# Second layer's expert feed-forward: tokens sorted through DRAM into 23 blocks, one expert each

## What is computed

```python
def _L1_ffn_ref(x, switch_w, switch_b, w1, b1, w2, b2):
    t = x.reshape(-1, d)                                # 2048 tokens of 128
    route_prob = jax.nn.softmax(t @ switch_w + switch_b, axis=-1)
    route_prob_max = jnp.max(route_prob, axis=-1)
    routes = jnp.argmax(route_prob, axis=-1)
    for e in range(8):                                  # w1[e]: 128 x 512, w2[e]: 512 x 128
        h = jax.nn.gelu(t @ w1[e] + b1[e])
        y = h @ w2[e] + b2[e]
        out = jnp.where((routes == e)[:, None], y, out)
    return out * route_prob_max[:, None]
```

## Time and profile before

| what | value |
|---|---|
| time, median of 3 runs | 1949.45 us (1949.03 to 1950.55) |
| profiled execution: span of its instructions | 1948.2 us |
| median less that span | 1.25 us |
| TensorE busy | 1760.2 us, 90% |
| VectorE busy | 1222.4 us, 63% |
| ScalarE busy | 966.7 us, 50% |
| POOL busy | 265.7 us, 14% |
| mean granted TensorE clock | 0.972 of 2.4 GHz |
| chain that ended last | TensorE 65%, VectorE 18%, ScalarE 7%, issue 7% |
| transfers, whole run | 21.09 MB, 3.6% of the sixteen DMA engines' time |

### The profile page before, as it was taken

The page is one execution under the profiler, slowest core; times in us unless marked ns, Lnnn a source line. Parts: engine busy times, 40 slices in busy tenths (PEclk is TensorE's granted clock), DMA queues, the critical chain, the costliest instruction groups (busy, mean ns, idle before and its releaser), DMA issues.

```text
span 1948.2 us, 40574 instructions
## 1 busy us (share of the span) xinstructions
PE 1760.2 (90%) x14281; PEld 1350.1 (69%) x14281; DVE 1222.4 (63%) x3198; ACT 966.7 (50%) x2010; POOL 265.7 (14%) x358
## 2 busy tenths in 40 slices
PE   4999999989997899988999977999968999999987
PEld 3788888866664688875777754666646777777775
DVE  5966666667665678884222246555555778777781
ACT  1566666654332567775444343323314556555552
POOL 2000000011002143321000014000010011111111
PEclk9999999999998899998999989999978999999999
DMA  8000000000002000000000010000000000000000
GB/s 251 1 1 0 0 0 0 0 2 1 1 0 64 27 1 0 0 1 1 1 1 0 0 51 1 1 1 0 0 0 1 1 1 0 0 0 0 0 1 22
DMA packets 19157, 21.09 MB, mean 11 GB/s; under 512 B 4650, under 2 KB 14003, under 8 KB 18884
## 3 DMA queue, kind: packets, MB, share of 16 engines
q1 hardware_dynamic: 19076, 20.02, 3.6%
HBM read 18.97 MB, written 1.05 MB: 10 GB/s over the span
## 4 chain that ended last, share of the span: by engine, by line
PE 65%; DVE 18%; ACT 7%; issue 7%; POOL 1%; SPq 1%; DMA 0%; DVEq 0%; ACTq 0%; POOLq 0%
PE bank L1152 56%; PE bank L1156 9%; DVE PTs L1754 2%; DVE negm L1745 2%; DVE negm L1750 2%; ACT Pm L1053 2%; DVE Qz L1949 2%; ACT VxF L1010 1%; ACT PTs L1009 1%; ACT Pm L1113 1%; DVE Qz L1549 1%; DVE VxF L604 1%; DVE st L1557 1%; DVE On L1810 1%; SPq L699 1%
## 5 line engine op out<-in xcount | busy, mean ns | idle before, releaser
L1152 PE MATMUL bank<-kT,Qz 128*128 128x256 f32 (+1 forms) x1568 | 442.3, 387 | 4.0 <-issue 1.6
L1053 ACT ACTIVATE Pm<-bank,negm 128x256 f32<-128x256 f32 x784 | 326.7, 468 | 207.0 <-DVE negm L1750 206.3
L1152 PE MATMUL bank<-xH,R 128*128 (+3 forms) x928 | 299.6, 382 | 13.5 <-DVE Qz L1949 13.4
L1152 PEld LDWEIGHTS bank<-R,Qz 128*128 128x128 f32 (+1 forms) x2496 | 293.8, 192 | 17.8 <-ACT Qz L1120 6.4
L1152 PE MATMUL bank<-R,Qz 128*128 128x128 f32 (+1 forms) x2496 | 295.2, 276 | 3.1 <-ACT Qz L1120 3.1
L1152 PEld LDWEIGHTS bank<-kT,Qz 128*128 128x128 f32 x1568 | 248.9, 192 | 67.9 <-issue 16.9
L1156 PE MATMUL bank<-ident,Pm 128*128 128x128 f32 x1568 | 239.1, 275 | 50.6 <-DVE PTs L1754 40.6
L1754 DVE TENSOR_TENSOR PTs<-bank,PTs 128x512 f16<-128x512 f32 x384 | 261.9, 682 | 7.7 <-ACT PTs L1009 7.2
L1156 PEld LDWEIGHTS bank<-ident,Pm 128*128 128x128 f32 x1568 | 187.2, 141 | 113.3 <-issue 59.2
L1750 DVE TENSOR_REDUCE negm<-bank 128x2 f32<-128x512 f32 x264 | 181.6, 688 | 95.6 <-PE bank L1152 91.7
L1009 ACT ACTIVATE PTs<-bank 128x512 f16<-128x512 f32 (+1 forms) x388 | 231.3, 596 | 3.1 <-PE bank L1156 3.1
(11 more groups left out here) (231 smaller groups left out, 2085.1 us busy)
## 6 DMA issues: line engine op xcount, KB each, us to landing
R<-in_L_ffn_ew SPq DMA_DIRECT2D x2, 1024.0 KB, 6.9
R<-in_L_ffn_w SPq DMA_DIRECT2D x1, 2048.0 KB, 9.8
R<-in_L_xattn_Wkv SPq DMA_DIRECT2D x2, 768.0 KB, 6.5
R<-in_L_ffn_w SPq DMA_DIRECT2D x1, 1408.0 KB, 12.9
R<-in_L_xattn_Wq SPq DMA_DIRECT2D x2, 512.0 KB, 3.7
out<-x SPq DMA_DIRECT2D x4, 256.0 KB, 2.3
PTs<-in_ctx SPq DMA_DIRECT2D x1, 768.0 KB, 8.1
R<-in_L_xattn_Wo SPq DMA_DIRECT2D x1, 512.0 KB, 7.8
```

The lines of the kernel that those rows point to most:

```text
L1053: last = act.activation(Pm[:, k % 4, qt * S:(qt + 1) * S], bank[k % 2][:, qt * S:(qt + 1) * S], ACT.Exp, bias=negm[:, k % 4, qt:qt + 1])
L1152: return pe.matmul(o, l, r, start=start, stop=stop)
```

## The change

The second layer's feed-forward (`ROUTED = (1,)`) no longer follows `ffn_schedule`. Each engine gets a function `routed` that runs once for all 2048 tokens:

1. Each attention sequence's normalised rows are also copied by POOL, unturned, to `xrow` (which takes the memory of `xH` and `xL`; the split of this layer's inputs goes).
2. TensorE makes the gate for all four chunks; VectorE finds each token's expert as a one-hot row. TensorE counts, with an upper triangular matrix and sums over tiles, each token's rank among those of its expert. VectorE rounds each expert's count up to whole blocks of 128 and so gets each token's slot, and each block's expert. 2048 tokens make at most 16 + 7 = 23 blocks.
3. The down bias is added for all tokens, through TensorE, into `x`. VectorE then takes the third layer's maxima (`layer2_scale`).
4. POOL scatters the 16 tiles of rows to DRAM (`xs`), by slot, in 16 indirect transfers.
5. SP loads the sorted rows block by block, up to eight ahead. For each block TensorE turns the rows, ScalarE and VectorE split them into f16 parts, TensorE multiplies them by the weights of the block's expert, ScalarE applies bias and gelu, TensorE makes the down product, VectorE copies it out, and SP stores it to DRAM (`ys`). The expert's number is loaded to a register of TensorE and of ScalarE, and the addresses of weights and bias are computed from it.
6. When all blocks are stored, POOL gathers 16 tiles of rows back by slot, VectorE adds them with the token's weight to `x`, and statistics, normalisation and turn go by chunks.

Around it: DRAM rows are zeroed by ten writes of 256 KB on SP's queue in the beginning, and POOL sets some more constants there. The third layer's `early` waits for the routed stage's semaphores.

```diff
+ROUTED = (1,)
+RING = 8
+def n_blocks(F):
+    return NT * F.k + 7
...
@@ sync
+            sp.wait_ge(consts_ready, 2)
+            for i in range(10):
+                sp.dma_start(xs[512 * i:512 * i + 512, :].rearrange("(t p) d -> p t d", p=P),
+                             wpad[:, :, :]).then_inc(rows_zeroed, 16)
...
+                def load_block(i):
+                    sp.wait_ge(r.turned, i - RING + 1) if i >= RING else None
+                    sp.dma_start(xb[:, i % RING, :], xs[i * P:(i + 1) * P, :]).then_inc(r.loaded[i % RING], 16)
+                sp.wait_ge(r.scattered, 16 * NT * F.k)
+                for i in range(RING):
+                    load_block(i)
+                for i in range(nb):
+                    sp.wait_ge(r.y_read, i + 1)
+                    sp.dma_start(ys[i * P:(i + 1) * P, :], yb[:, i % RING, :]).then_inc(r.stored[i % RING], 16)
+                    if i + RING < nb:
+                        load_block(i + RING)
@@ gpsimd, attention
+                    if A.n in ROUTED:
+                        need(pool, s.yn, b + 1)
+                        pool.tensor_copy(xrow[:, bass.ds(2 * b, 2), :], yn[:, 0:2, :]).then_inc(routed_s[A.n].rows, 1)
@@ gpsimd, feed_forward
+                if F.n in ROUTED:
+                    pool.memset(Vx2[:, :, 128], 1.0).then_inc(zeroed, 1)
+                    largest(2)
+                    routed(F)
+                    return
...
+            def routed(F):
+                pool.wait_ge(r.rows, B)
+                pool.wait_ge(r.slots, 1)
+                for t in range(NT):
+                    pool.indirect_dma_start(out=xs, out_offset=bass.IndirectOffsetOnAxis(ap=slotu[:, t:t + 1], axis=0),
+                                            in_=xrow[:, t, :], in_offset=None).then_inc(r.scattered, 16)
+                for j in range(RING):
+                    pool.wait_ge(r.stored[j], 16 * ((nb - j + RING - 1) // RING))
+                def gather(t):
+                    if t >= RING:
+                        pool.wait_ge(r.added, t - RING + 1)
+                    pool.indirect_dma_start(out=yg[:, t % RING, :], out_offset=None, in_=ys[0:nb * P, :],
+                                            in_offset=bass.IndirectOffsetOnAxis(ap=slotu[:, t:t + 1], axis=0)
+                                            ).then_inc(r.gathered[t % RING], 16)
+                for t in range(RING):
+                    gather(t)
+                for c in range(NCH):
+                    need(pool, s.lnf, c + 1)
+                    need(pool, s.stats, c + 1)
+                    normalise(4, s.stats, c + 1, s.yn, 1.0, EPS, link)
+                    for t in range(RING + 4 * c, min(RING + 4 * c + 4, NT)):
+                        gather(t)
@@ scalar, per block
+                        move(xbH[:, i % 4, :], bank[6 + i % 2][:, 0:P]).then_inc(r.high, 1)
+                    if i >= 1:
+                        j = i - 1
+                        e = act.value_load(blocke[0:1, j:j + 1], min_val=0, max_val=7)
+                        act.wait_ge(r.h, j + 1)
+                        for ft in range(F.FT):
+                            last = act.activation(sg[:, j % 4, ft * P:(ft + 1) * P],
+                                                  bank[j % 2][:, ft * P:(ft + 1) * P], ACT.Gelu_apprx_tanh,
+                                                  bias=vecT[:, bass.ds(e * 4 + (V_B1 + ft), 1)],
+                                                  scale=upback[:, 1:2])
@@ tensor
+                need(pe, att_s[F.n].yn, B)
+                for t in range(2):
+                    last = turn(bank[6][:, t * P:(t + 1) * P], yn[:, t, :])
+                last.then_inc(s.lnf.sem, 1)
...
+                def up_block(i):
+                    e = expert[i] = pe.value_load(blocke[0:1, i:i + 1], min_val=0, max_val=7)
+                    pe.wait_ge(r.high, i + 1)
+                    pe.wait_ge(r.low, i + 1)
...
+                    for ft in range(F.FT):
+                        o = bank[i % 2][:, ft * P:(ft + 1) * P]
+                        w = [r1h[:, bass.ds(e * 1024 + (512 * j + ft * P), P)] for j in range(2)]
+                        mm(o, w[0], xbH[:, i % 4, :], True, False)
+                        mm(o, w[0], xbL[:, i % 4, :], False, False)
+                        last = mm(o, w[1], xbH[:, i % 4, :], False, True)
+                def down_block(i):
+                    pe.wait_ge(r.g, i + 1)
+                    for ft in range(F.FT):
+                        last = mm(bank[4 + i % 2][:, 0:P], sg[:, i % 4, ft * P:(ft + 1) * P],
+                                  R1[:, bass.ds(e * 512 + (4608 + ft * P), P)], ft == 0, ft == F.FT - 1)
+                turn_block(0)
+                for i in range(nb + 1):
+                    if i + 1 < nb:
+                        turn_block(i + 1)
+                    if i < nb:
+                        up_block(i)
+                    if i:
+                        down_block(i - 1)
@@ vector
+                for c in range(NCH):
+                    dve.wait_ge(r.bias, c + 1)
+                    dve.tensor_tensor(x[:, 4 * c:4 * c + 4, :], bank[c % 2][:, :].rearrange("p (t d) -> p t d", d=D),
+                                      x[:, 4 * c:4 * c + 4, :], ALU.add).then_inc(r.bias_added, 1)
+                layer2_scale()
+                for i in range(nb + 1):
+                    if i < nb:
+                        dve.wait_ge(r.high, i + 1)
+                        dve.tensor_tensor(xbL[:, i % 4, :], bank[6 + i % 2][:, 0:P], xbH[:, i % 4, :],
+                                          ALU.subtract).then_inc(r.low, 1)
+                    if i:
...
+                        dve.tensor_copy(yb[:, j % RING, :], bank[4 + j % 2][:, 0:P]).then_inc(r.y_read, 1)
```

More of the change, by code:

```diff
@@ L66, in __init__ @@
         self.ctxb, self.qm, self.ostats, self.onorm = c["ctxb"], c["qm"], c["ostats"], c["onorm"]
+class RoutedSems:
+    def __init__(self, sem, n):
+        self.gate, self.gate_read, self.logits = sem(f"r{n}_gate"), sem(f"r{n}_gate_read"), sem(f"r{n}_logits")
+        self.onehot, self.rank, self.slots = sem(f"r{n}_onehot"), sem(f"r{n}_rank"), sem(f"r{n}_slots")
+        self.experts, self.shifted, self.exped = sem(f"r{n}_experts"), sem(f"r{n}_shifted"), sem(f"r{n}_exped")
+        self.w, self.wT, self.wT_read = sem(f"r{n}_w"), sem(f"r{n}_wT"), sem(f"r{n}_wT_read")
+        self.bias, self.bias_added = sem(f"r{n}_bias"), sem(f"r{n}_bias_added")
+        self.rows, self.scattered = sem(f"r{n}_rows"), sem(f"r{n}_scattered")
+        self.loaded = [sem(f"r{n}_loaded{j}") for j in range(RING)]
+        self.turned, self.high, self.low = sem(f"r{n}_turned"), sem(f"r{n}_high"), sem(f"r{n}_low")
+        self.h, self.g, self.y, self.y_read = sem(f"r{n}_h"), sem(f"r{n}_g"), sem(f"r{n}_y"), sem(f"r{n}_y_read")
+        self.stored = [sem(f"r{n}_stored{j}") for j in range(RING)]
+        self.gathered = [sem(f"r{n}_gathered{j}") for j in range(RING)]
+        self.added = sem(f"r{n}_added")
 class FeedForwardSems:
@@ L574, in build, with splits_before @@
                  counted(list(ffn_counts(FFN[0])), "ffn_", [ffn_counts(F) for F in FFN])]
+        routed_s = {n: RoutedSems(sem, n) for n in ROUTED}
+        def splits_before(n):
+            return sum(NCH for m in range(n) if m not in ROUTED)
         Vx2 = VxF[:, 0:16 * 129].rearrange("p (t e) -> p t e", e=129)
@@ L794, in _ @@
             pool.memset(mb3[:, :], 0.0)
-            pool.memset(wpad[:, :, :], 0.0)
+            pool.memset(onehot[:, :, :], 0.0)
+            pool.memset(before128[:, :, :], 128.0)
             for e in range(8):
                 pool.memset(iota[:, e:e + 1], float(e))
+                pool.memset(rev[:, e:e + 1], 8.0 - e)
+            for i in range(40):
+                pool.memset(step128[:, i:i + 1], 128.0 * i)
+            link(pool.memset(under[:, :], 1.0))
+            link(pool.affine_select(out=under[:, :], in_=under[:, :], compare_op=ALU.is_ge, fill=0.0,
+                                    base=-1, pattern=[[1, P]], channel_multiplier=-1))
+            pool.affine_select(out=before128[:, :, :], in_=before128[:, :, :], compare_op=ALU.is_ge, fill=0.0,
+                               base=-1, pattern=[[1, 8], [-1, 8]], channel_multiplier=0)
             link(pool.memset(headmask[:, :], 1.0))
@@ L880, in body @@
                             normalise(2, s.stats, h + 1, s.yn, 1.0, EPS, link, 2 * (h % 2))
-                            if h == 5:
+                            if h == 5 and A.n not in ROUTED:
                                 split_inputs(0)
@@ L904, in body @@
                         largest(A.n)
-                    if A.n < 2 and kinds == "last":
+                    if A.n < 2 and A.n not in ROUTED and kinds == "last":
                         m = [m for kind, k, m, _ in steps(A, b, kinds) if kind in FILLS][0]
@@ L1257, in attention @@
                     need(pe, f.lne, NCH)
-                    need(pe, f.gle, NCH)
-                    if FFN[A.n - 1].k == 1:
```

(19 more changed lines are left out.)

215 lines of the change are left out of this document (208 added, 7 removed).

## The result

The changed kernel takes 1907.38 us (median of 4 runs, 1906.42 to 1908.51), the kernel before 1950.0 beside it; the ratio is 0.978, 95% interval 0.977 to 0.980. Forecast were 1898, its own range 1880 to 1920, the wide one 1862 to 1942. The profiled execution has a span of 1904.9 us.

The account below looks back on a forecast made before the run. TensorE, nearly without a gap from 890.1 to 1114.86 us, was taken as the bound. Eleven dependent steps end at 1063.5, 51.4 sooner: 1949.45 - 51.4 + 0.3 = 1898.4, so 1898 us, range 1880 to 1920.

Parts of the forecast that it names:

- Steps 1 to 3: Stage start: last normalisation with gate products queued behind the turn, +4.4; gate, +8.1; routing on VectorE and TensorE, +7.8 us.
- Step 4: Down bias through TensorE: 1.9 us a chunk plus 1.5 of fill, +9.1 us.
- Step 5: Next layer's scale: POOL's reduction, behind VectorE's maxima, stands ahead of the scatter; 6.07 + 0.15, then 2.8, +9.1 us.
- Step 6: Scatter: 16 indirect transfers from POOL at 1.2 us each, 19.2, and 2.0 to land, +21.2 us.
- X: Price of one indirect transfer on POOL: taken as 1.2 us, from 0.79 for its own pass and 0.43 for an issue.
- cheap transfers: Rival: POOL's indirect transfer costs as an SP issue, 0.43 us, so 25 us less, 1873; chance 24%.
- slower case: Rival on POOL's queue: above 2.8 us per indirect transfer the change loses, at 3.34 the time is 1966; chance 11%.
- Step 8: Block loop: 23 blocks at 3.0 us, 69 plus 2.5 for fill and drain, +71.5 us.
- ScalarE's sum: Block pace set by ScalarE: 1.75 busy + 0.9 register load + 0.3 addresses = 3.0 us.
- Queue-bound or cold: Rival: TensorE's register load and addresses don't overlap, or it stays at 1.2 GHz: 4.6 to 5.2 us a block; 13%.
- Step 10: Gathers on POOL: 16 gathers, 19.2, and three normalisations, 13.9, ahead of the third chunk's turn, +33.3 us.
- Step 11: Third chunk's turn and ScalarE's copy, 1.3, then the next layer's fills at about half clock, +2.5 us.

Follow-up runs that it names:

- experiment 8: Changed kernel with the last batch's turn ahead of only the fourth gate product, on TensorE and ScalarE: 1904.22 us, ratio 0.977.
- experiment 1: Changed kernel with POOL's largest(2) reduction moved from ahead of the scatters to behind them: 1890.23 us, ratio 0.970.
- experiment 4: Changed kernel with ScalarE's register load and bias addresses per block replaced by constants: 1905.98 us.
- 5: Changed kernel with all 23 TensorE register loads ahead of the block loop: 1904.47 us, ratio 0.977.
- 6: Changed kernel with VectorE's f16 low part of the next block ahead of copying out the previous block: 1898.99 us, ratio 0.975.
- experiment 11: The kernel of 9 with TensorE's 23 register loads ahead of its block loop, the fastest: 1855.16 us, ratio 0.952.
- experiment 2: Changed kernel with constant weight addresses on TensorE, its register load per block kept: 1894.47 us.
- experiment 7: Changed kernel with two short spare POOL operations added behind the scatters: 1897.87 us, ratio 0.974.
- 9: The combined kernel: changed kernel with the edits of experiment 1, 6, experiment 7, experiment 8, and VectorE's reduction read behind its loop: 1866.25 us, ratio 0.958.

## Why the prediction was right or wrong

Ends of its steps, forecast and measured, of the profiled execution:

| step | forecast | measured |
|---|---|---|
| 1, 2: normalisation, gate | 894.5, 902.6 | 894.0, 902.2 |
| 3: routing | 910.4 | 909.1 |
| 4: bias | 919.5 | 921.5 |
| 5: scale, reduction | 928.6 | 928.6 |
| 6: scatters landed | 949.8 | 950.1 |
| 7: first block's turn | 952.2 | 952.1 |
| 8: blocks done | 1023.7 | 1027.0 |
| 9: first gather | 1026.4 | 1029.4 |
| 10: third chunk normalised | 1059.7 | 1070.7 |
| 11: the next layer's fill | 1063.5 | 1072.7 |

- **What goes and what bounds it.** Right: TensorE's work fell, and most of what was freed came back as waiting, in four stretches.
- **Steps 1 to 3** hold within 1.3. Experiment 8 shows that the queue's order in step 1 costs 3.2, not the whole 4.4, since the fourth gate product needs the rows in any case.
- **Step 4** was short by 3.2: 12.3 from routing's end to the last add. A chunk takes 2.95, as the first three adds do from one to the next in VectorE's timeline of the changed kernel:

```profile
908.84 0.29 DVE L2217 TENSOR_TENSOR OT<-onehot,OT 128x128 f32<-128x128 bf16 x1
913.18 0.69 DVE L2220 TENSOR_TENSOR x<-bank,x 128x512 f32<-128x512 f32 x1 [4.05 <-PE bank L1333]
916.13 0.69 DVE L2220 TENSOR_TENSOR x<-bank,x 128x512 f32<-128x512 f32 x1 [2.25 <-PE bank L1333]
```

  Four f32 products take 2.07 with the clock granted at 0.50, the 1.2 GHz level; the four turns of 1.0 stand before them on the same engine. I took 1.9 a chunk, which fits the full clock.
- **Step 5** was right in the place and 2.0 too dear in the price. The cover that was gone did cost 6.2 us of VectorE. But the reduction's result is there 0.6 us after the rows (927.64 to 928.20), not 2.8: the 2.8 I read from the earlier trace rows held a pause ahead of the reduction (5.67 idle with "issue" in that row), which I had taken for its latency. That step 5 ends at 928.6 as forecast is luck: +3.2 in step 4, -2.0 in step 5 and -1.3 up to step 3 cancel. Experiment 1 confirms that the order on POOL is what costs: undone, the scatter starts 20 us sooner, counted from attention's end.
- **Step 6.** X = 1.2 against 1.26, landing 2.0 against 2.2. The sum of POOL's own pass over 128x128 and an issue was near. Both rivals that turned on X are out: the cheap transfers need 0.43, the slower case 2.8.
- **Step 8, the size right, the reason wrong.** The pace is 3.03 against 3.0, and the loop 75 us against 71.5, since the first blocks run at the clock's lower level (granted 0.50 from 952 to 962, 1.00 from 967; TensorE had been 0.00 busy from 929 to 952). But ScalarE's sum does not set it: ScalarE is idle over 1 us a block, and experiment 4 is flat. What sets it is up products slowed by register addresses, 1.16, down 0.99, and 0.89 from turn to the next up, which two things fill, VectorE's ring and behind it TensorE's register load (experiments 5, 6 and 11). My half landing of 0.9 for the load was too dear: on ScalarE it is hidden, and on TensorE 23 loads in a row are 0.66 apart (experiment 11); with them gone from the loop of the combined kernel, turn to next up falls from 0.55 to 0.11 and the up products by 0.2. The Trainium skill (DMA: Bandwidth & Descriptors, section Latency and other measured facts) gives about 600 ns as the floor of such a load, and the 0.66 agrees with it.
- **The rule on pairs.** 0.055 us per product at full clock with constant addresses, as taken from the earlier trace rows. The 81 ns that the Trainium skill gives (TensorE: Matmul & The Clock Gate, section Back-to-back issue gap) is not a floor here, since twelve pairs in a row are 55 ns apart in experiment 2; with register addresses a pair takes more, 97 ns.
- **Queue-bound or cold.** This rival had the right place and too high a price: 4.6 to 5.2 a block were 3.03. The queue part is real, the cold part only in the first four blocks.
- **Step 10, the one that failed.** From first gather to third normalisation 41.3 against 33.3. Gathers are 1.25 apart and normalisations as priced; what is missing is the 7.1 us pause on POOL. Its sign stood in the timeline: 5.67 idle with "issue" ahead of the reduction, and 7.30 behind it (the row under experiment 7). I did not ask what either was. Of the 9.2 us between 51.4 and 42.2, the pause is 7.1 (shown by experiment 7), the block loop 3.4, the gathers about 1; step 11 gives 1.8 back, and steps 7 and 9 another 0.4. The term that failed is thus this step's +33.3, which put POOL's idle time ahead of the first normalisation at nothing.
- **Step 11 and the sum.** The fills do run at half clock, but that lies behind the first fill's start: from there to the next layer's first turn 11.8 us (1072.69 to 1084.52), 10.6 in the kernel before (1114.86 to 1125.44), so 1.2 where I had 2.5. From that turn to the end it is 820.4 us, 822.8 before, in layers that the change does not touch; these take 819.7 to 824.3 in the other profiles, so the 2.4 are luck. 42.2 - 1.2 + 2.4 = 43.4, and the spans differ by 43.3.
- **VectorE's copies beside the gathers**, the small sink among the rivals: the gather beside the first copy is 1.05 busy (1036.92), the others mostly 0.94. At 0.1 us each they cost nothing that counts.
- **At no cost**: right. The memsets of the setup left no trace at attention's end (0.5 sooner), and attention's stretches did not grow (TensorE busy 812.3 us up to 888, 810.9 before).

What stays open: why POOL pauses ahead of a partition reduction and behind it. That the pauses go with that instruction and with the first ordinary one behind it is shown by moving them (experiments 1 and 7); what the engine does in them isn't.

## What to carry to other kernels

Where a dense stage becomes a row of dependent steps, price the order of each queue, not only the engines: of the 52 us that the moves brought, some 31 were order alone (experiments 1, 6 and 8, and VectorE's read in 9). If taking out a suspect changes nothing, it may stand behind another of the same length: take out both before you acquit it, as the register load shows. Idle time marked "issue" on an engine off the path, in the trace of before, is a cost that a change can put on the path.

## What the hardware showed

- **POOL's pauses.** Ahead of the reduction over partitions POOL is idle 5.6 to 5.8 us, whether its rows come 0.7 us before POOL is free (experiment 1) or 3.3 after (the kernel before), so this is no wait for them. Another 6.8 to 7.8 stand ahead of the next ordinary operation (the next but one in the kernel before, where a cast is recorded right behind the reduction). It makes no difference whether that comes at once or 118 us later, with gathers and long waits between: those don't absorb it. In the changed kernel the first of the two hides in 33 us of waiting. The timeline of POOL of the fastest kernel has both, under the loop:

```profile
929.20 0.38 POOL L946 PARTITION_ALL_REDUCE uprowall<-uprow  x1 [5.68 <-issue]
936.61 0.19 POOL L1076 TENSOR_SCALAR spare<-spare 128x4 f32<-128x4 f32 x1 [7.03 <-issue]
```

- **Indirect transfers** of 128 rows cost POOL 1.26 us each (0.96 busy), scatter and gather alike, within 0.1 whatever VectorE did beside them here; they land 2.2 and 2.5 us after, as the DMA rows of the changed kernel say:

```profile
token_rows_by_expert<-xHL,slotu POOLq DMA_INDIRECT x16, 2.2
Qz<-expert_rows,slotu POOLq DMA_INDIRECT x16, 2.5
```

- **An address from a register** costs a 128-column f16 product 0.04 us on TensorE (experiment 2: twelve take 0.66 instead of 1.16); in experiment 11, with the loads out of the loop and the low part first, a bit over half of that (0.96). With the loads moved out but the ring still there (experiment 5) it stays 1.17. Why isn't shown.
- **A register load** on TensorE: 0.30 us by itself, 0.66 from one to the next (experiment 11). Per block it lay hidden behind a longer wait until that went.
